# MLP hidden columns moved to the place of the second expert matrices, those loaded in halves, and the last token tiles grouped three and one

## The chip, the cores and the metric

One core of one Trainium2 chip runs the whole program. The metric is the device time of one launch in microseconds (us), the median of several runs; lower is better. Engines are named as in the profile: PE is TensorE (matmuls; PEld its weight loads), DVE is VectorE, ACT is ScalarE, POOL is GpSimd, and SP is the engine that issues most DMAs.

## The reference, cut to what matters

Four batches of 1024 tokens with 256 channels pass through two layers. Layer 0 is softmax attention and a low-rank feed-forward; layer 1 is a linear-attention block with an MLP inside, and then a mixture of small experts. The change concerns the end of the layer-1 block and the start of the experts:

```python
# inside the layer-1 attention block
x = attn_out + inputs
y = layer_norm(x, ln2_scale, ln2_bias)
y = jax.nn.gelu(y @ w1 + b1) @ w2 + b2          # w1: 256x1024, w2: 1024x256
return x + y
...
# the experts: of each 16 consecutive tokens, each of 16*4 slots chooses one
grouped = x.reshape(x.shape[:-2] + (-1, ne, d))
logits = jnp.einsum('...btd,des->...btes', grouped, controller)
perm = (logits == jnp.max(logits, axis=-3, keepdims=True)).astype(x.dtype)
sel = jnp.einsum('...btd,...btes->...besd', grouped, perm)
inner = jax.nn.relu(jnp.einsum('...besd,desf->...besf', sel, f1) + bias)
inter = jnp.einsum('...besf,esfd->...besd', inner, f2)
out = jnp.einsum('...besd,...btes->...btd', inter, perm)
```

`f1` and `f2` are 4 MB each and are loaded anew for each batch. Between the MLP and the experts stands another normalisation with a per-batch scale and shift, applied to every token.

## The kernel before

`batch(b, carry)` writes out the work of one batch, in program order, into one list of steps per engine (`Lane.do`); `Lane.emit` then turns each list into instructions, and each step waits for the steps named as its predecessors. So each engine is strictly in order, and the order of the calls in `batch` is the order on every engine. SP's list holds DMA issues; all of them go to one hardware queue (q1 of the profile).

The 1024 tokens of a batch are 8 tiles of 128. `x`, `h` and `xn` hold token tiles [128 tokens, 256]. Two halves of 4 tiles are worked through one after the other in the MLP. Eight PSUM banks are handed out in rotation by `Banks.take()`; a bank may be taken again once the step given to `read_by` is done.

The stretch around the change, in program order with its lines:

- L1627: SP issues `load_f2` (L1493, two DMAs of 2 MB, each to 64 of the 128 partitions) once the last attention tile has been turned back. `f2` lies at the start of the slab (`OVERLAY`, 8 K words per partition).
- L1629 to L1638: `mlp_wide(half, ...)` makes the hidden columns `hid1` (1024 hidden channels as 8 blocks of 128 rows, by 512 tokens) with a GELU on ACT, `mlp_output(0, ...)` multiplies them by `w2` for tiles 0 to 3 and adds to `x` (`residual`, L1066 and L1068, both DVE), then `normalise`, `slot_rows_of` (DVE L1504, POOL L1506) and `mlp_wide(1, ...)`. `hid1` shares its memory with `sel`, the chosen rows, so no chosen row can be copied to `sel` before the last tile of the MLP has been multiplied.
- L1719 to L1752: tiles 4 to 7 of the MLP (`mlp_tile`, L1711, 8 products of 128x128 by 256, a generator that can be stopped in the middle) are mixed with the experts' choice for groups of tiles called LOW (0 to 3), MIDDLE (4, 5) and HIGH (6, 7). For each group: `norm_stats` (L297, L298, L300 on DVE, the power on POOL L301), `norm_apply` (L308), `slot_turn` (transposes L441, evacuated at L451 by ACT or L448 by DVE), `slot_rows_of`, `choices` (two products L470, three DVE passes L1521, L1525, L1526), `spread_choices` (transposes L1651, DVE L1655), `chosen_rows` for channel halves c=0 and c=1 (products L1685, copies to `sel` L1699 on ACT or L1701 on DVE; each call takes 4 banks) and `choice_blocks` (L1536). `hold_clock` puts spare transposes (L1667) on PE.
- L1758: SP issues `load_next`, the next batch's tokens `next_x` (two DMAs of 512 KB, to 128 partitions), once `choices(HIGH)` has been read from PSUM (`turned_read`). The last batch has none.
- L1763 to L1787: four blocks of the first expert product (L1773). After each block DVE adds the bias (L1779) and ACT takes the ReLU (L1786); after each addition, in the first three batches, DVE also takes the statistics of two tiles of `next_x` (L1784), which wait for all of `next_x`.
- L1790 to L1827: `rows_product(0)` and `rows_product(1)` (L1800), the first half of the second expert product; the first needs the ReLU of the first two blocks worked and all of `f2`, the second that of the last two. Then `second_product` (L1837), and the next batch's transposes.

The two statements in the stretch on which most hangs:

```python
            if b + 1 < NB:
                next_norm.update(norm_stats(next_x, n // 2, [NEXT_X] * 2, EPS, tiles=(2 * n, 2 * n + 1)))
...
            done = pe.do(emit, *[reader for i, ps, reader in taken.values()], inner_done[part_], inner_done[part_ + 2],
                         (loaded["f2"], 32 * (b + 1)))
```

Of the kernel before, what the change touches and what calls it, by code (L numbers as in the profile page):

```python
# [14 lines left out]
P = 128  # L15
NB = 4
S = 1024
# [95 lines left out]
def build(nc, I, out):  # L113
# [176 lines left out]
    def norm_stats(src, half, ready, eps, lanes=(dve, pool), filled=None, tiles=None):  # L290
# [4 lines left out]
        for pair, ready_ in zip(zip(tiles[0::2], tiles[1::2]), zip(ready[0::2], ready[1::2])):  # L295
# [3 lines left out]
            ts = slice(pair[0], pair[1] + 1, pair[1] - pair[0])  # L299
# [126 lines left out]
    def batch(b, carry):  # L426
# [671 lines left out]
        def gelu_into(dst, bias):  # L1098
            return lambda m, cols, ps, done: act.do(lambda e: nc.scalar.activation(
                dst[:, m, cols], ps, ACT.Gelu_apprx_tanh, bias=bias[:, m:m + 1]), done)  # L1100
# [347 lines left out]
        begin(WORK + 2 * S)  # L1448
        hid1 = part("hid1", [P, FM, S])
# [5 lines left out]
        def mlp_wide(half, turned):  # L1455
            return blocks(FM, lambda m, cols: [(w1[:, c, m * P:(m + 1) * P], mT[:, c, cols]) for c in range(C)], half, P,
                          gelu_into(hid1, b1_1), turned=turned)

        def mlp_output(half, wide, between=None):
            return to_residual(half, lambda tok: [(hid1[:, m, tok], w2[:, m, :]) for m in range(FM)], mod_rows[:, 4, :],  # L1460
                               wide=wide, ready=summed_x, between=between)

# [30 lines left out]
        def load_f2(e):  # L1493
            for k in range(2):
                last = e.dma_start(f2[k * EF:(k + 1) * EF, :, :], f2_dram[k]).then_inc(loaded["f2"], 16)
# [131 lines left out]
        sp.do(load_f2, last_turned)  # L1627
# [6 lines left out]
        LOW, MIDDLE, HIGH = tuple(range(TH)), (TH, TH + 1), (TH + 2, TH + 3)  # L1634
        mlp_turned = []
        slots_normed = [normalise(x, 0, mlp_output(0, wide0, lambda: mlp_turned.append(mlp_turn(1, mlp_norms[1]))), EPS)]
# [68 lines left out]
        def mlp_tile(t):  # L1705
# [4 lines left out]
            for m in range(FM):  # L1710
                done = pe.do(lambda e, m=m: nc.tensor.matmul(ps[:, 0:D], hid1[:, m, tok], w2[:, m, :], start=m == 0,  # L1711
# [6 lines left out]

        first_tile = mlp_tile(TH)  # L1719
# [4 lines left out]
        wrote4 = next(first_tile)  # L1724
        low_spread = spread_choices(LOW)
        *_, wrote5 = mlp_tile(TH + 1)
        middle_normed = norm_apply(x, norm_stats(x, 1, [wrote4, wrote5], EPS, tiles=MIDDLE))
        *_, wrote6 = mlp_tile(TH + 2)
        middle_turned = slot_turn(MIDDLE, middle_normed)
        middle_h = slot_rows_of(MIDDLE, middle_normed)  # L1730
        last_tile = mlp_tile(TH + 3)
        next(last_tile)
        choices(MIDDLE, middle_turned)
        wrote7 = next(last_tile)
        inv = norm_stats(x, 1, [wrote6, wrote7], EPS, tiles=HIGH)
        [*chosen_rows(LOW, (0,), [low_spread, *slots_h], ("act", "act", "act", "act"))]
# [229 lines left out]
```

## Time and profile before

| | us |
|---|---|
| median of 3 runs | 1734.58 (1732.05 to 1736.68) |
| the profiled execution | 1733.78 |
| its span | 1732.4 |

| engine | busy us | share of the span |
|---|---|---|
| PE | 1662.5 | 96% |
| PEld | 1133.2 | 65% |
| DVE | 1227.6 | 71% |
| POOL | 865.8 | 50% |
| ACT | 847.9 | 49% |

The profile divides the span among engines, gives the chain of work that ended last, and lists instructions by line. Shares of the whole span say little here: the four batches repeat one pattern of some 425 us, and the change touches some 40 us of each. The first expert product begins at 420.24, 845.64, 1271.11 and 1696.63 us of the span. All times quoted below are of the first batch unless said otherwise. "x4" behind a matmul line counts records; an fp32 product is recorded as two, a transpose as one.

### The profile page before, as it was taken

To read this page: it belongs to the slowest core of one execution; us is meant where nothing else is said; L and a number is where in the kernel's file an instruction comes from. 1 tells how busy PE (TensorE), PEld (TensorE's weight loads), DVE (VectorE), ACT (ScalarE), POOL (GpSimd) and SP (SyncE) were. 2 spreads that over 40 slices of the span, in tenths; PEclk is the share of its full clock that TensorE was granted. 3 is DMA by queue.
4 is the path that set the end of the run, shared out by engine and by line. 5 is a ranking of instruction groups with operands and counts; after the bars stand their busy time and mean duration, and the time that the engine had idled before them with its cause. 6 is when DMAs were issued, how large, how long until landed. Compare 5 with 4: busy or idle time off the path is not lost.

```text
span 1732.4 us, 41066 instructions
## 1 busy us (share of the span) xinstructions
PE 1662.5 (96%) x16518; PEld 1133.2 (65%) x16518; DVE 1227.6 (71%) x2678; ACT 847.9 (49%) x1864; POOL 865.8 (50%) x1123
## 2 busy tenths in 40 slices
PE   8999999999999999999999999999999999999997
PEld 5566685767566667566856667756684666766666
DVE  4988957626689994762678887675367999676545
ACT  5666634233577762422357765432245777443233
POOL 2788853141188884232128888314113888740410
PEclk9999999999999999999999999999999999999999
DMA  6566572141566655032346655405045666620504
GB/s 188 125 150 149 139 182 87 27 73 37 163 147 138 149 140 167 1 61 38 87 134 153 146 139 135 146 2 93 5 113 133 146 151 142 155 102 2 98 0 124
DMA packets 143853, 189.11 MB, mean 109 GB/s; under 512 B 34512, under 2 KB 107696, under 8 KB 142640
## 3 DMA queue, kind: packets, MB, share of 16 engines
q1 hardware_dynamic: 125472, 179.14, 42.1%
q10 hardware_dynamic: 18192, 7.35, 1.9%
q8 instruction: 131, 2.15, 0.6%
q14 instruction: 58, 0.48, 0.1%
HBM read 88.32 MB, written 13.16 MB: 59 GB/s over the span
## 4 chain that ended last, share of the span: by engine, by line
PE 61%; DVE 15%; ACT 6%; POOL 5%; SPq 5%; DMA 4%; issue 3%; POOLq 0%; ACTq 0%; DVEq 0%
PE scores L470 13%; PE bank L681 8%; PE scores L661 7%; SPq L1011 5%; PE bank L470 5%; DVE prob L800 5%; POOL placed L864 4%; DMA placed<-prob 4%; ACT prob L916 3%; PE bank L708 3%; PE scores L1711 2%; PE bank L718 2%; PE scores L1773 2%; PE scores L441 2%; PE scores L1368 1%
## 5 line engine op out<-in xcount | busy, mean ns | idle before, releaser
L864 POOL COPY placed<-prob 32x768 f32<-32x768 f32 x448 | 367.8, 821 | 216.7 <-DVE prob L800 186.0
L301 POOL TENSOR_TENSOR rstd<-rstd,minus_half 128x2 f32<-128x2 f32 x96 | 69.7, 728 | 506.9 <-DVE rstd L300 504.8
L681 PEld LDWEIGHTS bank<-placed,v_t 128*64 128x64 f32 x4608 | 250.7, 137 | 74.9 <-issue 73.2
L681 PE MATMUL bank<-placed,v_t 128*64 128x128 f32 x4608 | 272.6, 274 | 10.9 <-DMA placed<-prob 9.3
L661 PE MATMUL scores<-k_t,q_t 64*128 64x512 f32 (+3 forms) x1536 | 274.0, 496 | 1.1 <-DVE neg_max L793 1.0
L800 DVE STREAM_TRANSPOSE prob<-prob 128x1536 f32<-128x1536 f32 x128 | 222.5, 1764 | 46.7 <-ACT prob L916 46.5
L793 DVE CUSTOM_DVE_ANT_0 mod_rows<-scores,hx 128x128 f32<-128x128 f32 (+7 forms) x256 | 190.7, 745 | 32.1 <-PE scores L661 32.1
L661 PEld LDWEIGHTS scores<-k_t,q_t 64*128 64x128 f32 x1536 | 130.1, 187 | 112.9 <-issue 92.1
L864 POOL COPY placed<-hx 32x768 f32<-32x768 f32 x224 | 184.1, 822 | 33.3 <-DVE hx L800 16.6
L916 ACT ACTIVATE prob<-mod_rows,neg_max 128x128 f32<-128x128 f32 (+2 forms) x192 | 137.6, 717 | 117.6 <-DVE neg_max L793 113.9
L793 DVE CUSTOM_DVE_ANT_0 x<-scores,hx 128x128 f32<-128x128 f32 (+7 forms) x256 | 192.7, 753 | 0.0
L916 ACT ACTIVATE prob<-x,neg_max 128x128 f32<-128x128 f32 (+2 forms) x192 | 136.2, 709 | 0.0
L800 DVE STREAM_TRANSPOSE hx<-hx 128x1536 f32<-128x1536 f32 x64 | 112.0, 1749 | 6.1 <-ACT hx L916 6.1
L874 POOL TENSOR_TENSOR yT<-yT,inverse_wide 128x256 f32<-128x256 f32 (+2 forms) x128 | 91.4, 728 | 27.9 <-DMA inverse_wide<-inverse_scratch 21.4
L708 PE MATMUL bank<-hT,w_ring 128*64 128x512 f32 x448 | 101.5, 594 | 0.0
L1066 DVE TENSOR_TENSOR tmp<-bank,mod_rows 128x256 f32<-128x256 f32 x24 | 10.2, 424 | 125.8 <-PE bank L1122 71.5
L916 ACT ACTIVATE hx<-mod_rows,neg_max 128x640 f32<-128x640 f32 x64 | 59.9, 936 | 71.2 <-DVE neg_max L793 71.2
L470 PE MATMUL scores<-mT,w 128*128 128x512 f32 x192 | 85.4, 594 | 1.7 <-ACT mT L451 1.7
L924 ACT COPY yT<-bank 128x256 f32<-128x256 f32 (+2 forms) x128 | 44.1, 370 | 80.9 <-PE bank L681 80.7
L718 PE MATMUL bank<-w_ring,latT 128*64 128x128 f32 x1024 | 67.4, 275 | 3.4 <-ACT k_t L902 2.7
L451 ACT ACTIVATE hT<-scores,mod_cols 128x512 f32<-128x512 f32 (+1 forms) x40 | 26.8, 710 | 88.6 <-PE scores L441 88.6
L718 PEld LDWEIGHTS bank<-w_ring,latT 128*64 128x64 f32 x1024 | 57.2, 137 | 16.1 <-ACT k_t L902 8.9
(252 smaller groups left out, 3111.4 us busy)
## 6 DMA issues: line engine op xcount, KB each, us to landing
placed<-prob SPq DMA_DIRECT2D x576, 96.0 KB, 2.5
f<-in_L_ffn_f SPq DMA_DIRECT2D x16, 2048.0 KB, 13.6
placed<-hx SPq DMA_DIRECT2D x288, 96.0 KB, 2.2
inverse_wide<-inverse_scratch SPq DMA_DIRECT2D x64, 256.0 KB, 4.3
slots_scratch<-high_rows SPq DMA_DIRECT2D x16, 512.0 KB, 6.6
inter<-slots_scratch SPq DMA_DIRECT2D x32, 256.0 KB, 4.7
mod_rows<-mod_scratch SPq DMA_DIRECT2D x32, 128.0 KB, 5.0
out<-x SPq DMA_DIRECT2D x16, 256.0 KB, 2.1
```

The lines of the kernel that those rows point to most:

```text
L301: step = pool.do(lambda e, ts=ts: nc.gpsimd.tensor_tensor(rstd[:, ts], rstd[:, ts], minus_half[:, ts], op=ALU.pow), var, filled)
L470: step = pe.do(lambda e, n=n, w=w, m=m: nc.tensor.matmul(ps, w, m, start=n == 0, stop=n == len(pieces) - 1), copy, *after)
L661: last = nc.tensor.matmul(score_tiles[head][:, at_ // 512, at_ % 512:at_ % 512 + hi - lo], q_t[buf][rows_, tile * P:(tile + 1) * P], k_t[b ...
L681: last = nc.tensor.matmul(out_bank[rows_, at_:at_ + P], v_t[pair % 2][:, j, rows_], placed[m % 2][:, :, head, first_block(m, i) + j, :], s ...
L708: last = nc.tensor.matmul(ps[side, :], ring[:, c * P + side.start:c * P + side.stop], hT[:, c, cols], start=c == 0, stop=c == C - 1)
L718: last = nc.tensor.matmul(ps[side, t * P:(t + 1) * P], latT[:, at_ + side.start:at_ + side.stop], ring[:, 3 * P:4 * P], start=True, stop=True)
L793: nc.vector.tensor_tensor_reduce(masked_scores[head][:, cols], score_tiles[head][:, :, :].rearrange("p a n -> p (a n)")[:, cols], future[: ...
L800: nc.vector.transpose(p_, p_).then_inc(flow["shuffled"], 1)
L864: nc.gpsimd.tensor_copy(placed[m % 2][target * GROUP:(target + 1) * GROUP, source, :, :, :], prob[m % 3][source * GROUP:(source + 1) * GRO ...
L874: last = nc.gpsimd.tensor_tensor(dst, dst, out_place(m, lo, hi, inverse_wide), op=ALU.mult)
L916: nc.scalar.activation(prob[m % 3][:, :, head, blocks_in(m, i), :], masked_scores[head][:, columns_in(m, i)].rearrange("p (n g i) -> p g n ...
L1011: e.dma_start(placed[m % 2][target * GROUP:(target + 1) * GROUP, source, :, :, :], prob[m % 3][source * GROUP:(source + 1) * GROUP, target ...
```

## The change

`hid1` moves from the place of `sel` to that of `f2` and is laid out by halves. `f2` is loaded in two halves of its slots (4 DMAs of 1 MB instead of 2 of 2 MB): the first half after tile 3's MLP output, the second after that of tile 7. The chosen rows of tiles 0 to 3 for c=0 are multiplied and copied between the two halves of tile 6's MLP product, those for c=1 after `choices(MIDDLE)`. MIDDLE becomes tiles 4, 5, 6 and HIGH tile 7; HIGH's two channel halves come in one call. `choice_blocks(MIDDLE)` moves behind all chosen rows.

```diff
@@ norm_stats
-        for pair, ready_ in zip(zip(tiles[0::2], tiles[1::2]), zip(ready[0::2], ready[1::2])):
+        for pair, ready_ in [(tiles[k:k + 2], ready[k:k + 2]) for k in range(0, len(tiles), 2)]:
...
-            ts = slice(pair[0], pair[1] + 1, pair[1] - pair[0])
+            ts = slice(pair[0], pair[-1] + 1, max(pair[-1] - pair[0], 1))
@@ hid1
-        begin(WORK + 2 * S)
-        hid1 = part("hid1", [P, FM, S])
+        begin(OVERLAY)
+        hid1 = part("hid1", [P, NH, FM, HW])
+        begin(WORK + 10 * S)
         mT = part("mT", [P, C, S])
...
+        def mlp_hidden(m, tok):
+            half, at_ = tok.start // HW, tok.start % HW
+            return hid1[:, half, m, at_:at_ + P]
@@ load_f2
-        def load_f2(e):
+        def load_f2(e, half):
+            qs = slice(half * EP // 2, (half + 1) * EP // 2)
             for k in range(2):
-                last = e.dma_start(f2[k * EF:(k + 1) * EF, :, :], f2_dram[k]).then_inc(loaded["f2"], 16)
+                last = e.dma_start(f2[k * EF:(k + 1) * EF, qs, :], f2_dram[k][:, qs, :]).then_inc(loaded["f2"], 16)
             return last
@@ after the attention
-        sp.do(load_f2, last_turned)
...
-        LOW, MIDDLE, HIGH = tuple(range(TH)), (TH, TH + 1), (TH + 2, TH + 3)
+        LOW, MIDDLE, HIGH = tuple(range(TH)), (TH, TH + 1, TH + 2), (TH + 3,)
         mlp_turned = []
-        slots_normed = [normalise(x, 0, mlp_output(0, wide0, lambda: mlp_turned.append(mlp_turn(1, mlp_norms[1]))), EPS)]
+        outputs0 = mlp_output(0, wide0, lambda: mlp_turned.append(mlp_turn(1, mlp_norms[1])))
+        low_output = outputs0[-1]
+        slots_normed = [normalise(x, 0, outputs0, EPS)]
@@ the tiles 4 to 7
+        sp.do(lambda e: load_f2(e, 0), low_output)
         first_tile = mlp_tile(TH)
         next(first_tile)
         choices(LOW, low_turned)
         choice_blocks(LOW)
         act.do(lambda e: nc.scalar.activation(spare_column[:, :], minus_half[:, 0:1], ACT.Exp))
         wrote4 = next(first_tile)
+        *_, wrote5 = mlp_tile(TH + 1)
+        inv = norm_stats(x, 1, [wrote4, wrote5], EPS, tiles=MIDDLE[0:2])
         low_spread = spread_choices(LOW)
-        *_, wrote5 = mlp_tile(TH + 1)
-        middle_normed = norm_apply(x, norm_stats(x, 1, [wrote4, wrote5], EPS, tiles=MIDDLE))
-        *_, wrote6 = mlp_tile(TH + 2)
+        middle_normed = norm_apply(x, inv)
+        third_tile = mlp_tile(TH + 2)
+        next(third_tile)
+        [*chosen_rows(LOW, (0,), [low_spread, *slots_h], ("act", "act", "act", "act"))]
+        wrote6 = next(third_tile)
+        middle_normed += norm_apply(x, norm_stats(x, 1, [wrote6], EPS, tiles=MIDDLE[2:]))
+        last_tile = mlp_tile(TH + 3)
+        next(last_tile)
         middle_turned = slot_turn(MIDDLE, middle_normed)
         middle_h = slot_rows_of(MIDDLE, middle_normed)
-        last_tile = mlp_tile(TH + 3)
-        next(last_tile)
+        wrote7 = next(last_tile)
+        sp.do(lambda e: load_f2(e, 1), wrote7)
+        inv = norm_stats(x, 1, [wrote7], EPS, tiles=HIGH)
         choices(MIDDLE, middle_turned)
-        wrote7 = next(last_tile)
-        inv = norm_stats(x, 1, [wrote6, wrote7], EPS, tiles=HIGH)
-        [*chosen_rows(LOW, (0,), [low_spread, *slots_h], ("act", "act", "act", "act"))]
+        [*chosen_rows(LOW, (1,), [], ("act", "act", "act", "act"))]
+        high_normed = norm_apply(x, inv)
         middle_spread = spread_choices(MIDDLE)
-        choice_blocks(MIDDLE)
-        high_normed = norm_apply(x, inv)
-        second_low = chosen_rows(LOW, (1,), [], ("act", "act", "act", "act"))
-        next(second_low)
         high_turned = slot_turn(HIGH, high_normed, shared=True)
         high_h = slot_rows_of(HIGH, high_normed)
-        [*second_low]
+        [*chosen_rows(MIDDLE, (0,), [middle_spread, *middle_h], ("act", "act", "act", "dve"))]
         turned_read = choices(HIGH, high_turned)
-        middle_rows = chosen_rows(MIDDLE, (0, 1), [middle_spread, *middle_h], ("act", "act", "dve", "dve"))
+        middle_rows = chosen_rows(MIDDLE, (1,), [], ("act", "act", "act", "dve"))
         next(middle_rows)
         high_spread = spread_choices(HIGH)
         [*middle_rows]
-        [*chosen_rows(HIGH, (0,), [high_spread, *high_h], ("act", "dve", "act", "dve"), held=6)]
-        [*chosen_rows(HIGH, (1,), [], ("dve", "act", "dve", "act"))]
+        [*chosen_rows(HIGH, (0, 1), [high_spread, *high_h], ("act", "dve", "act", "dve"), held=6)]
+        choice_blocks(MIDDLE)
         choice_blocks(HIGH)
@@ rows_product
-                         (loaded["f2"], 32 * (b + 1)))
+                         (loaded["f2"], 64 * (b + 1)))
```

## Rows read from the trace of the kernel before

**Rows 1.** The page: busy tenths and granted clock in 40 slices

```profile
PE   8999999999999999999999999999999999999997
PEclk9999999999999999999999999999999999999999
```

**Rows 2.** Chain of work, MLP tiles to first expert product: start us, us, what

```profile
395.56 0.46 PE scores L1651 x4
396.01 7.10 PE scores L1711 x32
...
408.39 0.43 DVE tmp L1066
408.85 0.42 DVE x L1068
409.27 0.35 DVE stats L297
...
410.63 0.71 POOL rstd L301
411.37 0.42 DVE hx L308
...
418.05 0.38 PE scores L1685 x2
...
420.24 7.61 PE scores L1773 x256
427.86 1.03 PE scores L1800 x32
...
431.51 1.93 PE scores L1837 x32
```

**Rows 3.** Timeline of PE: start us, us, engine, line, what, idle before

```profile
388.84 1.04 PE L441 MATMUL scores<-ident,hx 128*128 128x128 f32 x8
389.72 1.89 PE L1711 MATMUL bank<-w,hid 128*128 128x256 f32 x8
409.38 0.33 PE L1651 MATMUL scores<-ident,permT 64*128 64x64 f32 x2
```

**Rows 4.** Timeline of DVE in the same stretch

```profile
396.86 0.68 DVE L1655 TENSOR_TENSOR perm<-scores,par_mask 128x512 f32<-128x512 f32 x1
...
414.31 0.42 DVE L1521 TENSOR_TENSOR logits<-scores,tie 128x256 f32<-128x256 f32 x1 [0.35 <-PE scores L470]
```

**Rows 5.** Timeline of ACT: copies of the chosen rows of tiles 0-3

```profile
410.00 1.57 ACT L1699 COPY sel<-scores 128x512 f32<-128x512 f32 x3
```

**Rows 6.** Issues by SP's queue: start us, us, line, what

```profile
339.66 2.62 SPq L1495 DMA_DIRECT2D f<-in_L_ffn_f  x2
414.76 0.94 SPq L271 DMA_DIRECT2D next_x<-in_L_attn_x  x2
```

**Rows 7.** Issue to landing: f2's two DMAs, then next_x's two

```profile
DMA to landing us min/median/max: 13.6/18.8/24.1
...
DMA to landing us min/median/max: 4.5/5.0/5.5
```

**Rows 8.** Stretches of f2's stream and next_x's: ..., clock, DMA share, GB/s

```profile
353.00:363.00 10.00, 10.00 (x30) 5.51 (x29) 0.13 (x1) 3.44 (x5) 7.12 (x10) 1.00 1.10 184
417.00:418.00 1.00, 0.71 (x16) 0.52 (x16) 1.00 (x4) 0.35 (x2) 0.00 (x0) 1.00 1.07 369
```

**Rows 9.** Timelines of DVE and ACT beside the first expert product

```profile
422.91 0.42 DVE L297 BATCH_NORM_STATS2 stats<-next_x 128x6 f32<-128x256 f32 x1
...
424.19 0.68 DVE L1779 TENSOR_TENSOR hx<-scores,fbias 128x512 f32<-128x512 f32 x1
...
428.65 0.63 ACT L1786 ACTIVATE inner<-hx 128x512 f32<-128x512 f32 x1 [1.24 <-DVE hx L1779]
```

**Rows 10.** A longer idle of PE, last batch: timeline, then a stretch's granted clock

```profile
1722.02 1.67 PE L1895 MATMUL scores<-inter,blockT 128*32 128x256 f32 x16 [2.15 <-DMA inter<-slots_scratch]
...
1723.00:1724.00 1.00, 0.68 (x8) 0.00 (x0) 0.27 (x1) 0.00 (x0) 0.00 (x0) 0.50 1.14 329
```

More of the change, by code:

```diff
@@ L1096, in blocks, with gelu_into @@
             return res
-        def gelu_into(dst, bias):
+        def gelu_into(dst, bias, place):
             return lambda m, cols, ps, done: act.do(lambda e: nc.scalar.activation(
-                dst[:, m, cols], ps, ACT.Gelu_apprx_tanh, bias=bias[:, m:m + 1]), done)
+                dst[:, m, place], ps, ACT.Gelu_apprx_tanh, bias=bias[:, m:m + 1]), done)
         def modulated_rows(half, inv, scale, shift):
@@ L1456, in mlp_wide @@
             return blocks(FM, lambda m, cols: [(w1[:, c, m * P:(m + 1) * P], mT[:, c, cols]) for c in range(C)], half, P,
-                          gelu_into(hid1, b1_1), turned=turned)
+                          gelu_into(hid1[:, half, :, :], b1_1, slice(0, HW)), turned=turned)
         def mlp_output(half, wide, between=None):
-            return to_residual(half, lambda tok: [(hid1[:, m, tok], w2[:, m, :]) for m in range(FM)], mod_rows[:, 4, :],
+            return to_residual(half, lambda tok: [(mlp_hidden(m, tok), w2[:, m, :]) for m in range(FM)], mod_rows[:, 4, :],
                                wide=wide, ready=summed_x, between=between)
+        def mlp_hidden(m, tok):
+            half, at_ = tok.start // HW, tok.start % HW
+            return hid1[:, half, m, at_:at_ + P]
         begin(OVERLAY)
@@ L1710, in mlp_tile @@
             for m in range(FM):
-                done = pe.do(lambda e, m=m: nc.tensor.matmul(ps[:, 0:D], hid1[:, m, tok], w2[:, m, :], start=m == 0,
+                done = pe.do(lambda e, m=m: nc.tensor.matmul(ps[:, 0:D], mlp_hidden(m, tok), w2[:, m, :], start=m == 0,
                                                              stop=m == FM - 1), reader, wide1[m])
```

## The prediction

> **What bounds the kernel now.** The page comes first: PE is busy nine tenths or more in nearly every slice, at full granted clock [rows 1], so time is to be had only where PE stands still or does spare work. The chain of waits is read next, for the stretch that the change touches. In it, the reader is to see two parts. From 396.01 to 408.36 us PE's MLP products carry the chain. From 408.39 to 420.24 us, from the last MLP product to the first expert product, it runs through small steps of four engines: residual, statistics, the power on POOL, the normalisation, transposes, choice, spread, chosen rows, copies [rows 2]. I call this the tail; it lasts 11.9 us, and four batches have it. Behind it PE alone sets the pace: first expert product 7.6 us, the two row products 3.65 us, then the second product, from 431.51 us [rows 2]. That second part has two conditions that cost nothing today: all of f2 has landed long ago, since its issue was at 339.66 us [rows 6] and its slower DMA landed 24.1 us after its own issue [rows 7], and next_x, issued at 414.76 us [rows 6], has landed at the latest 5.5 us after its issue [rows 7], about 420.7 us, when DVE first reads it at 422.91 us [rows 9]. The slack is 2.2 us. SP's queue must be read for these, not the engines' busy time.
>
> **The tail, step by step** (first batch; the start at 389.88 us is unmoved). Prices: half a tile's product 1.73 us (396.01 to 403.12 is two tiles in 7.1 us) [rows 2, 3]; a transpose 0.11 (8 in 0.87 from 388.84 us) [rows 3]; 16 row products 1.02 (408.36 to 409.38 us) [rows 2, 3]; from an MLP product's end to the written tile 0.90 (408.36 to 409.27 us) [rows 2]; a pair's statistics up to POOL's start 1.36 (409.27 to 410.63), for one tile 0.35 + 0.19 less, 0.82 [rows 2]; POOL and the hand-over 0.74, a normalisation 0.42 [rows 2]; a DVE pass 0.68 for 512 columns and 0.42 for 256 [rows 4], so 0.55 for 384 and 0.29 for 128 by the same slope, an estimate. The change keeps all products; it reorders them.
>
> Tile 4 ends at 395.07 us, tile 5 follows at once and ends at 398.52. Its rows are written at 399.42, the pair's statistics are done at 400.73, and only then does DVE's queue reach the spread of LOW's choice, which ends at 401.41. PE has meanwhile done the spread's transposes (0.44) and half of tile 6, until 400.7: it stands 0.7 us for the spread, a new wait. Behind it in PE's queue stand the LOW products and the rest of tile 6; ACT is the only one to wait for them. LOW c=0 ends at 402.45, tile 6 at 404.2, written at 405.1, normalised at 405.1 + 0.82 + 0.74 + 0.42 = 407.1. Half of tile 7 ends at 405.93, then MIDDLE's six transposes wait for tile 6: a second new wait of 1.1 us. They end at 407.55, tile 7 at 409.28, and it is written at 410.2 us, 0.9 us later than before. One LOW group of 1.02 us and one wait of 1.1 have come in ahead of it, MIDDLE's choice of 0.86 has gone behind it.
>
> The rest is shorter. Statistics of one tile and the power end at 411.7. DVE is then in MIDDLE's choice (three passes of 384 columns, 410.95 to 412.7), so the normalisation ends at 413.05, not at 412.1. ACT copies LOW c=1 from 411.7 to 413.8 (four copies at 0.52) [rows 5], then the HIGH transposes' first half until 414.25. MIDDLE's spread on DVE ends at 413.7, its c=0 products at 414.5, HIGH's choice on PE at 414.9. DVE first copies its share of MIDDLE (until 415.2), then makes the three passes of HIGH at 128 columns: 415.5 is where HIGH's logits are read, 416.1 where the choice stands. Spread transposes 0.3, DVE 0.3; the HIGH products start at 417.0. From the last group's start to the first expert product took 2.19 us (418.05 to 420.24) [rows 2] for as many products and the 12 spare transposes; that stays, as the copies (four of 128 columns on each of two engines, some 0.9 us) fit under it. So the first expert product starts at F = 419.2 us, 1.0 us earlier. The copying of LOW is no longer in the tail, but ACT was not what the tail waited for; the chain's small steps are, and their number is unchanged. MIDDLE's three copies on ACT cost nothing while they hide beside HIGH's choice. The later choice_blocks hide under the first expert product; uncovered they would cost under 1 us. The new layout of hid1 has the same rows and strides within a product: nothing, and 0.1 us per batch either way at the most, since its 8 products and GELUs keep their shapes.
>
> **The loads.** f2's first half is issued at some 378 us with SP idle and no user for 40 us: free. The second half can't be issued before tile 7 is written, at 410.2 us, 70 us later than all of f2 today. 2 MB on this path take 13.6 us to landing (f2's first DMA) [rows 7]; the stream behind it runs at 184 GB/s with all engines busy [rows 8]. Two DMAs of 1 MB keep 64 partitions and 1 KB pieces, so I take 13.6: landed at 423.85 us. The row products need it at F + 7.6 = 426.8: 3 us to spare. Bounds: 8.5 us if it flowed like next_x (369 GB/s) [rows 8], 14.7 with another issue.
>
> Next_x is what is late next. SP issues it behind f2, at 415.5 us, when 8 us of f2 are still in the queue. The two f2 DMAs landed one after the other (13.6 and 24.1 us) [rows 7], so a queue's DMAs go in order, and next_x lands 1.05 MB at 369 to 389 GB/s, 2.75 us, behind f2: N = 426.6 us. In three of four batches DVE's statistics of next_x stand between the first and second bias addition. DVE would be there at F + 2.67 = 421.9 us [rows 2, 9] and waits 4.7 us. Queued behind on DVE are the other three bias additions, hence ACT's ReLUs, hence both row products, hence PE. From DVE's first statistics to the last ReLU's end it is 6.37 us (422.91 to 429.28) [rows 9]; the second row product starts at N + 6.4 and ends 1.75 later, N + 8.15 = 434.75 us, where before it ended at 431.51 [rows 2]: 3.24 us per batch. What follows is paced by PE, so nothing gives it back. The last batch has no next_x and gains 1.0.
>
> The Trainium skill (SBUF — State Buffer, Door 1: The DMA port swizzle) says that partitions 0 to 63 reach only half of the 16 ports on SBUF's DMA side, and so do 64 to 127; half rate is what the trace shows. By its figure (half of 436 GB/s, an estimate) 2 MB would take 9.6 us where the trace has 11, and the sum would be 4.5 us less. The skill (DMA: Bandwidth & Descriptors, Queues, rings and completion order) adds that each DMA engine takes one queue's descriptors in ring order but alternates between queues; by that rule, with which the two landings agree, next_x would escape only from another queue, and the change has it on SP's.
>
> **Sum.** 3 x 3.24 - 1.04 = +8.7 us on the profiled execution's 1733.8: 1742.5. That execution lies 0.8 us under the median, so 1743.3.
>
> **Rivals.** (1) *The second half of f2 is early enough*: faster side. The point is fixed: next_x must land before 421.9 us, so f2 within 8.9 us of its issue. For it: smaller DMAs, next_x's rate of 369 GB/s, or next_x overtaking inside the queue. Against it: four batches' f2 loads all behaved alike, at half that rate. Then 4 x 1.04 is gained: 1730.4. (2) *The tail gains nothing*: if the new PE waits and ACT's queue eat the 1.0 us, only the last batch changes, as N does not depend on F: 3 x 3.24 = 9.7, 1744.3; it would also mean that the LOW copies between MLP tiles don't shorten anything. (3) *PE's clock falls*: PE idles 2.4 us ahead of the first row product. After an idle of 2.15 us the granted clock was 0.50 (1.2 GHz) a microsecond later [rows 10]. The first row product at half speed would only fill the wait for the last ReLU; I take 1 us more per batch: 1746.3. (4) *Better than reckoned ahead*: had I overstated the two new PE waits by 0.9 us, tile 7 is written at 409.3, N falls by 0.9, F is 2 us earlier: 3 x 2.34 - 2.0 = +5.0, 1739.6.
>
> **How the numbers follow.** Chances: the forecast 0.55, (1) 0.20, (2) 0.07, (3) 0.08, (4) 0.10. This kernel's measurement can tell about 0.3%, 5.2 us, from no change: bounds 1729.4 and 1739.8. Slower: 0.51 of the forecast's 0.55 (the rest if N is over 1.2 us earlier), (2), (3), 0.02 of (4): 0.68. Same: 0.04 + 0.08 of (1) + 0.08 of (4) = 0.20. Faster: 0.12, the part of (1) in which the tail gains over 1.3 us. The range reaches from 1731 (most of rival 1) to 1747 (rival 3); the forecast's own is 1739 to 1746.
>
> **What would show it.** In the profile after: tile 7 written near 410.2 and the first expert product near 419.2 us; PE idle ahead of the half-transposes of MIDDLE; f2's last DMA landing near 424, next_x's 11 us after its issue; DVE waiting some 4.7 us for a DMA ahead of L1784's statistics in three batches, not in the fourth; PE idle ahead of both row products, released by ACT. Wrong it is if DVE's statistics of next_x follow the bias addition at once, or if PE's waits ahead of the row products end with f2's DMA.

## The result, and the profile after

The changed kernel takes 1751.41 us (median of 4 runs, 1750.16 to 1754.31) against 1734.58 us of before: 16.8 us more, and the recorded ratio is 1.0102, interval 1.0089 to 1.0114. (Before's number is the median of three runs; a fourth, of 2135.92 us, fell in a slower state that the chip has and is left out.) It is slower by about twice what was forecast. Its profiled execution took 1750.16 us, span 1748.8 us.

The page of the changed kernel, engines' busy time, granted clock by slices and PE's instruction queue (packets, MB, share):

```profile
PE 1670.0 (95%) x16518; PEld 1140.5 (65%) x16518; DVE 1227.3 (70%) x2674; ACT 851.4 (49%) x1872; POOL 868.1 (50%) x1127
...
PEclk9999999999999999999999999999999999999998
...
q8 instruction: 131, 2.15, 0.5%
```

PE has as many matmuls as before and is busy 7.5 us longer, so some of them ran slower; the other 9 us of the span are idle time. The page says no more than that. The stretch of the first batch on PE, to be held against [rows 2, 3] (by the chain of work its tile 4 starts at 385.63 us, that of before at 389.88; the timelines have both some 0.17 us earlier):

```profile
397.10 0.39 PE L1692 MATMUL scores<-perm,hx 32*128 32x128 f32 x3 [0.53 <-DVE perm L1662]
...
403.11 0.66 PE L441 MATMUL scores<-ident,hx 128*128 128x128 f32 x4 [0.97 <-DVE hx L308]
...
409.07 0.37 PE L1658 MATMUL bank<-ident,permT 64*128 64x64 f32 x3 [1.18 <-DVE permT L1532]
...
412.98 0.88 PE L1674 MATMUL scores<-ident 128*128 128x128 f32 x6
...
415.90 0.97 PE L1784 MATMUL scores<-sel,f 128*64 128x64 f32 x25
419.29 8.62 PE L1784 MATMUL scores<-sel,f 128*64 128x64 f32 x231 [2.41 <-issue]
427.84 1.10 PE L1811 MATMUL scores<-f,inner 64*64 64x128 f32 x32
...
430.17 1.98 PE L1811 MATMUL scores<-f,inner 64*64 64x128 f32 x64 [0.36 <-ACT inner L1797]
432.08 2.00 PE L1848 MATMUL scores<-inner,f 64*128 64x64 f32 x32
```

The first three are the new idles of the reordering; two were foreseen. The line at 419.29 was not: after 25 records of the first expert product PE stands 2.41 us with "issue" as the reason, that is, for nothing that a semaphore shows. Behind it 231 records take 8.6 us, where before 256 took 7.6 [rows 2]. The wait for the last ReLU, which the prediction made the whole loss, is there too, at 430.17, with 0.36 us. Small as it is, it is the wait that ends last in this batch: the chain of work, followed back from the second product, doesn't go through PE's idle but through next_x.

```profile
412.48 11.15 DMA next_x<-in_L_attn_x
...
423.65 0.44 DVE stats L297
...
429.40 0.64 ACT inner L1797
...
430.17 1.98 PE scores L1811 x64
```

The second batch shows PE's idle larger, and with it the clock (stretches: busy time of PE, PEld, DVE, ACT, POOL, then granted clock, DMA share, GB/s):

```profile
845.83 2.49 PE L1784 MATMUL scores<-sel,f 128*64 128x64 f32 x77
852.20 7.01 PE L1784 MATMUL scores<-sel,f 128*64 128x64 f32 x179 [3.88 <-issue]
...
850.00:852.00 2.00, 0.00 (x0) 0.00 (x0) 0.00 (x0) 0.00 (x0) 0.00 (x0) 1.00 0.98 314
...
854.00:855.00 1.00, 1.00 (x24) 1.00 (x22) 0.93 (x4) 0.00 (x0) 0.00 (x0) 0.50 0.00 0
```

PE stands 3.88 us while the DMA engines are full, and works on at a granted clock of 0.50 (1.2 GHz), as it did behind the idle of [rows 10]. The 179 records took 7.0 us where before they took 5.3: 1.7 us more. Here the chain does go through the idle:

```profile
848.32 3.88 issue
852.20 7.01 PE scores L1784 x179
859.21 1.03 PE scores L1811 x32
```

DVE and SP's queue, to be held against [rows 6, 7, 9]: next_x waited for in the first and second batch; the issues of f2's second half and next_x; issue to landing of f2's four DMAs of the first batch and of next_x's in all three:

```profile
423.65 0.43 DVE L297 BATCH_NORM_STATS2 stats<-next_x 128x6 f32<-128x256 f32 x1 [1.42 <-DMA next_x<-in_L_attn_x]
...
853.88 0.43 DVE L297 BATCH_NORM_STATS2 stats<-next_x 128x6 f32<-128x256 f32 x1 [5.22 <-DMA next_x<-in_L_attn_x]
...
406.44 1.31 SPq L1501 DMA_DIRECT2D f<-in_L_ffn_f  x2
412.04 0.94 SPq L271 DMA_DIRECT2D next_x<-in_L_attn_x  x2
...
DMA to landing us min/median/max: 8.0/10.3/13.8
...
DMA to landing us min/median/max: 8.8/10.2/11.5
```

next_x does land behind f2, at 423.62 us, and DVE does wait for it. That all four batches lose can be seen in one table, worked out from the timelines of PE (us; A is the start of tile 4's product, F the first expert product, R the first row product, E the second product):

| | F - A | R - F | E - R | E - A | PE idle in the first product |
|---|---|---|---|---|---|
| before, batches 1, 2, 4 | 30.45 | 7.6 | 3.65 | 41.72 | 0 |
| after, batch 1 | 30.44 | 11.94 | 4.24 | 46.62 | 2.41 |
| after, batch 2 | 30.43 | 13.31 | 3.65 | 47.39 | 3.88 |
| after, batch 3 | 33.17 | 9.88 | 3.66 | 46.71 | 1.95 |
| after, batch 4 | 31.70 | 8.70 | 3.65 | 44.05 | 0.82 |

(Before's third batch has 41.94.) The losses in E - A are 4.9, 5.7, 4.8 and 2.3 us, together 17.7. By columns that is 13.4 us in the first product (9.1 of idle, 4.3 of slower records), 4.0 in the tails of batches 3 and 4, and 0.4 in the row products. The stretches between the batches' changed parts are 0.7 us longer in sum and the end of the program 2.3 us; against that this execution reached its first tile 4 4.3 us earlier. That last is luck: over all the profiles of this case tile 4 starts anywhere from 385.5 to 389.7 us, whether f2 is loaded early or late. 17.7 + 0.7 + 2.3 - 4.3 = 16.4 us, the difference of the spans.

**Where PE stops.** If PE stands for want of instructions, the idle must lie at fixed places of its program. Queue q8 of the page carried 131 packets of instructions, 2.15 MB, so 16 KB each; PE has 33,574 records (weight loads, matmuls and the few others), which is 131 times 256 and 38 more. I numbered the records in the order of the trace and took each idle put down to issue inside the first expert product ("remainder" is what is left of the number when divided by 256):

| kernel | batch | idle us | records ahead of it | remainder by 256 |
|---|---|---|---|---|
| after | 1 / 2 / 3 / 4 | 2.41 / 3.88 / 1.95 / 0.82 | 7361 / 15809 / 24257 / 32449 | 193 / 193 / 193 / 193 |
| loads_only | 1 / 2 / 3 / 4 | 2.96 / 2.58 / 3.11 / 2.14 | 7361 / 15809 / 24257 / 32449 | 193 / 193 / 193 / 193 |
| narrow_beside | 1 / 2 / 3 | 3.21 / 1.50 / 2.55 | 7617 / 16065 / 24257 | 193 / 193 / 193 |
| wide_beside | 1 / 2 / 3 | 0.74 / 0.94 / 2.00 | 7617 / 16065 / 24257 | 193 / 193 / 193 |

Fourteen idles in four different kernels, and all at the same remainder: they are the borders of blocks of 256 instructions. PE has used up its blocks there and the next has not come. The other experiments with a stream beside the first product (two_queues, late_statistics and next_x_late) have eight more, all at remainder 193.

The trace also holds the packets of q8, and they show the block coming. In all 22 cases PE goes on 1.2 to 1.6 us after one such packet has ended: at 419.28 us after the packet of 416.29 to 417.70, at 852.20 after that of 849.66 to 850.79. These packets took 1.0 to 1.5 us, no longer than those of the kernel before (0.9 to 1.65). So the block isn't moved slowly; it starts late. In the kernel before, the packet that belongs to a border inside the first product had ended 1.4 to 4.0 us ahead of it: the spare time was thin already. The Trainium skill (Runtime: NRT & Kernel Launch, Instruction fetch mechanics) describes such blocks of 16 KiB, 256 instructions, fetched by DMA while the ones before are executed, and calls their cost mostly hidden. The traces agree on the block; hidden it is only as long as the DMA engines are free.

### The profile page after: what moved, and what is told of

It is laid out like the page before. It is cut to its first block, busy times and chain, and to the rows that moved or that the text cites. A ratio compares the mean times of both kernels' runs of the same rounds, so it can differ in the third digit from the quotient of the medians.

```text
span 1748.8 us, 41074 instructions
## 1 busy us (share of the span) xinstructions
PE 1670.0 (95%) x16518; PEld 1140.5 (65%) x16518; DVE 1227.3 (70%) x2674; ACT 851.4 (49%) x1872; POOL 868.1 (50%) x1127
## 3 DMA queue, kind: packets, MB, share of 16 engines
q8 instruction: 131, 2.15, 0.5%
## 4 chain that ended last, share of the span: by engine, by line
PE 64%; DVE 15%; ACT 5%; SPq 5%; POOL 4%; DMA 4%; issue 3%; ACTq 0%; POOLq 0%; DVEq 0%
PE scores L470 13%; PE bank L681 9%; PE scores L661 7%; PE bank L470 5%; SPq L1011 4%; DVE prob L800 4%; ACT prob L916 3%; POOL placed L864 3%; PE bank L708 2%; DMA placed<-prob 2%; PE bank L718 2%; PE bank L712 2%; DVE stats L297 2%; DVE hx L800 2%; PE scores L1784 1%
## 5 line engine op out<-in xcount | busy, mean ns | idle before, releaser
L301 POOL TENSOR_TENSOR rstd<-rstd,minus_half 128x2 f32<-128x2 f32 (+1 forms) x100 | 71.5, 716 | 523.1 <-DVE rstd L300 521.0
L1066 DVE TENSOR_TENSOR tmp<-bank,mod_rows 128x256 f32<-128x256 f32 x28 | 11.9, 423 | 128.7 <-PE bank L1122 70.7
L708 PEld LDWEIGHTS bank<-hT,w_ring 128*64 128x64 f32 x448 | 31.6, 137 | 53.3 <-issue 53.3
## 6 DMA issues: line engine op xcount, KB each, us to landing
f<-in_L_ffn_f SPq DMA_DIRECT2D x8, 2048.0 KB, 11.5
```

The costliest lines, as they stand in the source:

```text
L301: step = pool.do(lambda e, ts=ts: nc.gpsimd.tensor_tensor(rstd[:, ts], rstd[:, ts], minus_half[:, ts], op=ALU.pow), var, filled)
L708: last = nc.tensor.matmul(ps[side, :], ring[:, c * P + side.start:c * P + side.stop], hT[:, c, cols], start=c == 0, stop=c == C - 1)
```

## The experiments

Ratios are to before, measured beside each. The theories at the start: LOADS, in two parts (NEXT_X, the predicted wait, and STARVATION, PE without instructions), against ORDER.

**order_only**: the new order of the tiles, without the late load.

```diff
-        begin(OVERLAY)
+        begin(WORK + 2 * S)
         hid1 = part("hid1", [P, NH, FM, HW])
...
+        sp.do(load_f2, last_turned)
-        sp.do(lambda e: load_f2(e, 0), low_output)
-        sp.do(lambda e: load_f2(e, 1), wrote7)
```

> The changed order of the tiles and chosen rows alone: the MLP's hidden columns lie by halves in the place of the chosen rows, as before (half 0 where channel half c=0 of them goes, so it can be written between MLP tiles), and f2 is loaded whole and early, as before. Theory LOADS (the late second half of f2 costs everything: next_x queued behind it, and PE short of instructions while the stream runs): 1735 to 1737 us, PE idle nowhere inside the first expert product. Theory ORDER (PE's new idle of 1.2 us ahead of MIDDLE's spread lowers the clock, as seen in batches 3 and 4 of the change): 1738 to 1741 us, with a granted clock near 0.5 in the tail.

Measured 1738.48 us, ratio 1.0014 (1.0002 to 1.0026), 10 runs. E - A is 41.73, 42.94, 41.72 and 41.73 us, no idle in the first expert product. So the order neither gains nor costs in three batches; in the second one PE was busy 1.6 of the 3 us from 836, a gap of 1.2 us among them, and the clock fell in the tail:

```profile
840.00:841.00 1.00, 1.00 (x17) 0.86 (x20) 0.68 (x3) 0.44 (x2) 0.00 (x0) 0.50 0.06 16
```

The median lies in theory ORDER's range, and the fallen clock is what ORDER said; but it is 2.7 us of a loss of some 17, so LOADS must account for nearly all.

**loads_only**: the order of before, hidden columns in f2's place, f2 in halves.

```diff
-        sp.do(load_f2, last_turned)
+        sp.do(lambda e: load_f2(e, 0), low_output)
...
         wrote7 = next(last_tile)
+        sp.do(lambda e: load_f2(e, 1), wrote7)
```

> The order of before, with hidden columns in f2's place and f2 loaded in halves, the second after tile 7's output. Theory LOADS: tile 7 is written 1.4 us earlier than in the change, f2 and next_x need some 17 us from there, so the second product starts some 3.5 us late in three batches, or later where PE runs short of instructions: 1745 to 1750 us, idle of 1 to 4 us put down to issue inside the first expert product in all four batches. Theory ORDER: 1735 to 1740 us.

Measured 1750.84 us, ratio 1.009 (1.0073 to 1.0107), just above the range of LOADS. F - A is 30.46 in all batches, so nothing is lost ahead of the first product; E - A is 45.33, 46.07, 45.52 and 44.19. In the first batch:

```profile
419.45 0.92 PE L1782 MATMUL scores<-sel,f 128*64 128x64 f32 x24
423.32 6.99 PE L1782 MATMUL scores<-sel,f 128*64 128x64 f32 x232 [2.96 <-issue]
```

The loads alone make nearly the whole loss, the last batch (which has no next_x) with 2.5 us too. That batch can't be NEXT_X's. The first three could: their second products start 8.5, 9.3 and 9.3 us behind next_x's landing, and next_x_late below measures what that wait takes by itself, 8.46 us.

**no_second_half**: the change without the second load (the products read f2's first half in its place, so half of the second matrices is left out).

```diff
-        sp.do(lambda e: load_f2(e, 1), wrote7)
...
-                                                         inner[rows_, q, :], f2[rows_, q, P:D], start=True, stop=True)
+                                                         inner[rows_, q, :], f2[rows_, q % (EP // 2), P:D], start=True, stop=True)
```

> The change without the load of f2's second half; the products read the first half in its place (it leaves out half of the second expert matrices). Both parts of theory LOADS: 1735 to 1738 us, next_x landing 5 us after its issue, no idle inside the first expert product. If the stream of f2 is not the cause: still near 1751 us.

Measured 1738.83 us, ratio 1.0019 (1.0009 to 1.0029): the same as order_only. E - A is 41.73, 42.94, 42.99, 41.72; next_x lands 3.8 to 5.5 us behind its issue again. The stream is the cause. Two batches lose the 1.2 us of the clock, which puts the time 0.8 us over the expected range.

**late_statistics**: the change with next_x's statistics out of the bias additions' way.

```diff
-            if b + 1 < NB:
-                next_norm.update(norm_stats(next_x, n // 2, [NEXT_X] * 2, EPS, tiles=(2 * n, 2 * n + 1)))
...
         for part_ in range(2):
             rows_product(part_)
+            for n in (2 * part_, 2 * part_ + 1) if b + 1 < NB else ():
+                next_norm.update(norm_stats(next_x, n // 2, [NEXT_X] * 2, EPS, tiles=(2 * n, 2 * n + 1)))
```

> The change with the statistics of next_x moved behind the row products' copies, so that no bias addition waits for next_x. If the wait for next_x carries the loss, as predicted: 3 x 3 to 5 us less than the change, 1737 to 1742 us. If PE's idle inside the first expert product (2.4, 3.9, 2.0 and 0.8 us in the change's trace) and the halved clock behind it carry it, the wait for next_x being hidden under them: only 0.5 to 2 us less than the change, 1749 to 1751 us.

Measured 1760.76 us, ratio 1.0144: 9 us slower than the change, outside both expectations. E - A is 46.06, 47.42, 47.49 and 43.99 against the change's 46.62, 47.39, 46.71 and 44.05: taking the wait for next_x away gives nothing, as PE's own idle beside it is as long (five idles at block borders, 11.1 us in sum). The loss came behind it: from the second product to the next batch's tile 4 the three stretches are 4.6, 3.2 and 4.3 us longer than in the change. Of that 1.2 us is PE waiting for the normalisation on DVE ahead of the next batch's transposes (8.0 against 6.8 us ahead of L441); the rest was not traced. The experiment settles what it was for, E - A; as a repair it is none.

**next_x_late**: before, with next_x issued some 7.5 us later and no other stream.

```diff
-            sp.do(load_next, turned_read)
...
+            if n == 0 and b + 1 < NB:
+                sp.do(load_next, done)
```

> The kernel before with next_x issued once PE has done the first block of the first expert product, some 7.4 us later than before and with no f2 stream: the price of a late next_x by itself. Its landing is then some 5 us behind the issue, N = F + 7.1 against F + 2.67 where DVE wants it. Theory NEXT_X (the prediction's chain holds: DVE, bias additions, ReLUs, row products): the second product starts at F + 15.2 to 15.9 instead of F + 11.3 in three batches, not in the fourth: 1746 to 1750 us, PE idle ahead of the row products. If the chain has slack that the prediction missed: under 1740 us.

Measured 1752.61 us, ratio 1.0096 (1.0074 to 1.0117), above the expected range. In the first batch, on DVE and on PE:

```profile
426.87 0.43 DVE L297 BATCH_NORM_STATS2 stats<-next_x 128x6 f32<-128x256 f32 x1 [4.58 <-DMA next_x<-in_L_attn_x]
...
429.60 1.10 PE L1798 MATMUL scores<-f,inner 64*64 64x128 f32 x32 [2.45 <-ACT inner L1784]
...
433.39 1.98 PE L1798 MATMUL scores<-f,inner 64*64 64x128 f32 x64 [1.81 <-ACT inner L1784]
435.30 2.00 PE L1835 MATMUL scores<-inner,f 64*128 64x64 f32 x32
```

This is the predicted chain undisturbed: next_x waited for, both row products released by ACT's ReLUs, E - A 46.30, 47.14 and 46.24 us, the last batch 41.73. In all three batches the second product starts 8.46 us behind next_x's landing (the prediction said 8.15). The mechanism and its price hold.

With that number the change can be taken apart. next_x landed at 423.62, 853.86 and 1284.83 us; 8.46 us behind, the second product could start at 432.1, 862.3 and 1293.3, and it did at 432.08, 862.79 and 1294.12. So in the first batch the wait for next_x ended last and PE's idle was hidden beside it; in the second and third PE itself was later, by 0.5 and 0.8 us (in the third the tail, 2.7 us late, has its share). The wait alone would have cost 4.9, 5.2 and 3.9 us (an estimate, landing plus 8.46 against before), and late_statistics shows that without it PE's idle costs about as much: its E - F is 14.3, 17.0 and 15.8 us in these batches, against 11.3 before. Two causes, each nearly enough for the whole loss of these batches, ran side by side.

Two things more stand in this trace. In the third batch PE stands 1.19 us at a block border: a late next_x by itself is a stream that can starve it. And in the second batch the granted clock fell to 0.50 at the end of PE's idle of 3.30 us ahead of the first row product, the place that rival 3 named, yet the second product started 8.46 us behind the landing there too: it cost nothing ahead of it.

**narrow_beside** and **wide_beside**: before, with 1 MB more read into dead rows beside the first expert product in the first three batches, to 64 partitions at a time (narrow, the first DMA below) or to 128 (wide, the second).

```diff
             sp.do(load_next, turned_read)
+            sp.do(load_beside, sel_product[-1])
...
+        def load_beside(e):
+            for k in range(2):
+                last = e.dma_start(h[k * EF:(k + 1) * EF, :, :], f2_dram[k][:, 0:T, :]).then_inc(loaded["beside"], 16)
...
+                last = e.dma_start(h[:, ts, :], x_in[b][:, ts, :]).then_inc(loaded["beside"], 16)
```

> The kernel before with 1 MB of f2 read once more, to 64 partitions at a time, into the then dead rows of h, issued behind next_x once the last chosen rows are multiplied, so that it streams some 5.5 us beside the first expert product; only the next batch's clearing of that place waits for it. Theory STARVATION (a stream on the DMA engines keeps PE's instructions away by itself): idle of 1 to 3 us inside the first expert product in each batch, no engine waiting for a semaphore there, 1741 to 1750 us. If only waits for next_x and f2 cost: 1735 to 1737 us.

> The same as narrow_beside with 1 MB written to all 128 partitions (the rows that next_x also reads), which flows twice as fast. Theory STARVATION by a stream held up at its destination: little or no idle in the first expert product, 1735 to 1738 us. If any busy DMA engines starve PE: idle of about half of narrow_beside's, 1738 to 1743 us.

Measured 1744.86 us, ratio 1.005 (1.0035 to 1.0066), and 1738.61 us, ratio 1.002 (1.0009 to 1.0031). No step of the first product waits for the extra megabyte, and next_x lands as before; yet PE stands in the first expert product, here the first batch of each:

```profile
417.80 3.38 PE L1779 MATMUL scores<-sel,f 128*64 128x64 f32 x110
424.39 4.66 PE L1779 MATMUL scores<-sel,f 128*64 128x64 f32 x104 [3.21 <-issue]
```

```profile
424.32 3.25 PE L1780 MATMUL scores<-sel,f 128*64 128x64 f32 x104 [0.74 <-issue]
```

The idles are 3.21, 1.50 and 2.55 us narrow and 0.74, 0.94 and 2.00 us wide; the fourth batch, without the extra load, has none. (The profiled execution of wide_beside was the slowest of its ten, 1743.54 us, so its idles may be more than usual.) A stream by itself starves PE, and for longer when it is the narrow one, which lands 7.6 to 8.9 us behind its issue against 5.2 to 6.7. The rival (only a stream held up at its destination does it) falls: the wide one does it too.

**two_queues**: the change with the upper half's DMA issued by ACT.

```diff
-        sp.do(lambda e: load_f2(e, 1), wrote7)
+        sp.do(lambda e: load_f2(e, 1, (0,)), wrote7)
+        act.do(lambda e: load_f2(e, 1, (1,)), wrote7)
```

> The change, but of the second half of f2 the DMA for partitions 64 to 127 is issued from ACT's queue, the one for 0 to 63 from SP's, both once tile 7 is written. If a stream to 64 partitions is held at 190 GB/s by the place it writes to, the two together flow at up to 380 GB/s, f2 is in after 8 us instead of 13.6, next_x with it, and PE has its instructions again before the first expert product: 1737 to 1742 us. If the rate is set by how f2 is read, nothing changes: 1749 to 1752 us.

Measured 1743.35 us, ratio 1.0052 (1.0031 to 1.0073): half of the loss is gone, a little less than expected. f2's two DMAs of the first batch, and a stretch in which both flow:

```profile
DMA to landing us min/median/max: 8.0/10.0/11.9
...
414.00:417.00 3.00, 2.79 (x40) 2.29 (x33) 1.83 (x8) 2.02 (x7) 0.00 (x0) 1.00 1.12 275
```

The last landing is at 11.9 us instead of 13.8, next_x lands 6.2 to 8.6 us behind its issue instead of 8.8 to 11.5, and the idles in the first product are 0.88, 0, 0.76 and 0. That stretch has some of next_x in it; from 412.0 to 413.6 us, ahead of next_x's issue, f2's two DMAs alone had 292 GB/s. The stream in one queue stays at 194 to 201 GB/s in the change. One queue isn't the limit either, as next_x gets 369 GB/s in one [rows 8]. So the narrow stream is limited by the partitions that it writes. E - A is still 2.2 to 2.7 us over before in three batches.

**order_held**: order_only, 8 spare transposes in the gap ahead of MIDDLE's spread.

```diff
-        middle_spread = spread_choices(MIDDLE)
+        middle_spread = spread_choices(MIDDLE, held=8)
```

> order_only with 8 spare transposes of PE in the 1.35 us gap ahead of MIDDLE's spread, so that PE has no idle there. Theory CLOCK (the 1.2 us that one batch of order_only and two of no_second_half lost ahead of the first expert product, and the 2.7 and 1.3 us of the change's third and fourth batch, are that gap's): all four batches reach the first expert product 30.4 to 30.6 us after tile 4's start with the granted clock at 1.00, and the median falls by 1 to 3 us, to 1735 to 1737.5 us. Otherwise: one or two batches still late, 1738 to 1739 us.

Measured 1733.84 us, ratio 0.9989 (0.998 to 0.9999): 4.6 us under order_only by the medians, more than expected and more than the 1.2 us that order_only's one trace shows at this place. F - A is 30.38 or 30.39 in all four batches, so the 1.2 us of single batches, and the 2.7 and 1.3 us of the change's third and fourth, belong to the gap: in the change the third batch ran its tail at 0.50 from 1273 us on. The gap is in every batch, the lower clock only in some.

**retuned** and **retuned_less_held**: order_only, with the chosen rows of tiles 0-3 and the MIDDLE transposes behind tile 7, 8 or 2 spare transposes ahead of MIDDLE's spread, and 3 instead of 6 ahead of HIGH's products. Against order_only:

```diff
-        third_tile = mlp_tile(TH + 2)
-        next(third_tile)
-        [*chosen_rows(LOW, (0,), [low_spread, *slots_h], ("act", "act", "act", "act"))]
-        wrote6 = next(third_tile)
+        *_, wrote6 = mlp_tile(TH + 2)
...
         last_tile = mlp_tile(TH + 3)
         next(last_tile)
-        middle_turned = slot_turn(MIDDLE, middle_normed)
         middle_h = slot_rows_of(MIDDLE, middle_normed)
         wrote7 = next(last_tile)
         inv = norm_stats(x, 1, [wrote7], EPS, tiles=HIGH)
-        choices(MIDDLE, middle_turned)
-        [*chosen_rows(LOW, (1,), [], ("act", "act", "act", "act"))]
+        middle_turned = slot_turn(MIDDLE, middle_normed)
         high_normed = norm_apply(x, inv)
-        middle_spread = spread_choices(MIDDLE)
-        high_turned = slot_turn(HIGH, high_normed, shared=True)
+        [*chosen_rows(LOW, (0,), [low_spread, *slots_h], ("act", "act", "act", "act"))]
+        choices(MIDDLE, middle_turned)
+        second_low = chosen_rows(LOW, (1,), [], ("act", "act", "act", "act"))
+        high_turned = slot_turn(HIGH, high_normed)
         high_h = slot_rows_of(HIGH, high_normed)
-        [*chosen_rows(MIDDLE, (0,), [middle_spread, *middle_h], ("act", "act", "act", "dve"))]
+        [*second_low]
+        middle_spread = spread_choices(MIDDLE, held=8)
         turned_read = choices(HIGH, high_turned)
+        [*chosen_rows(MIDDLE, (0,), [middle_spread, *middle_h], ("act", "act", "act", "dve"))]
...
-        [*chosen_rows(HIGH, (0, 1), [high_spread, *high_h], ("act", "dve", "act", "dve"), held=6)]
+        [*chosen_rows(HIGH, (0, 1), [high_spread, *high_h], ("act", "dve", "act", "dve"), held=3)]
```

> The groups of 3 and 1 tiles on top of order_only (f2 whole and early, hidden columns by halves in the chosen rows' place), with the chosen rows of tiles 0-3 put back behind tile 7, where PE only waited for the normalisation, the MIDDLE transposes behind tile 7 too, and 8 spare transposes ahead of MIDDLE's spread. By the rows of before, PE loses no time ahead of tile 7 (written 1.6 us earlier than before, 3 us earlier than in the change), and the tail keeps its shortening by one tile: the first expert product 2 to 3.4 us earlier than before in all four batches: 1722 to 1728 us. If the tail's gain is illusory: 1733 to 1736 us.

> retuned with 2 instead of 8 spare transposes ahead of MIDDLE's spread. In retuned DVE waited 1.01 us for that spread, whose transposes stood behind the 8 spare ones although the choice was there. The spread comes some 0.7 us earlier, and everything behind it: first expert product 27.8 to 28.0 us after tile 4's start instead of 28.55, 1722 to 1724 us. If another wait takes its place (ACT's copies of tiles 0-3): 28.3 to 28.55 us and no change, 1724 to 1726 us.

Measured 1725.23 us, ratio 0.9945 (0.9927 to 0.9962), and 1725.73 us, ratio 0.9936 (0.992 to 0.9953): both beat before and the change. How much of it the three spare transposes left out ahead of HIGH's products give was not measured by itself. In retuned, tile 7's product ends 16.3 us after A (before 18.6, after 20.0) and F - A is 28.55 in all batches; the first expert product runs through:

```profile
416.09 7.68 PE L1783 MATMUL scores<-sel,f 128*64 128x64 f32 x256
```

With fewer spare transposes F - A is 27.9, within the expectation, and the profiled span is 1723.3 us against 1726.3; but the median is where it was, above the expected 1722 to 1724 us, and the two medians don't tell the versions apart.

## Why the prediction was wrong

The direction was right, the size half of the measured: +8.7 us forecast, +16.8 by the medians and +17.7 by the ratio and by the table of E - A. Three steps of the sum failed. The first is the size of the wait for next_x: three batches at 3.24 us, 9.7 in sum, where the measured landings make it 4.9, 5.2 and 3.9, 14.0 in sum. The second is a term that it had at nothing: PE's own supply of instructions. It adds little to these three batches only because it runs beside the wait; taking the wait away gave nothing back. The third is the last batch, forecast 1.0 us faster and 2.3 slower. The missing 9.0 us are 4.3 of the first, 1.3 by which PE was later than the wait in batches 2 and 3, and 3.4 of the last batch.

- **The tail.** Forecast: first expert product 1.0 us earlier. Measured: 0.0 in batches 1 and 2 (30.44 against 30.45), later in 3 and 4. The step that failed is the sum of small terms: tile 7 was written 20.8 us after tile 4's start, not 20.3 (the LOW group took 1.17, not 1.02, and the half tile behind it 1.94, not 1.73), HIGH's choice stood 27.0 us after it, not 26.2, and the HIGH products didn't wait for DVE's spread (done at 413.38) but for their own 6 spare transposes, which stood behind it in PE's queue (412.98 to 413.79 in the trace after); these I had left out. Rival 2 was nearer.
- **The idles of the reordering** were named, two of three with the right size (0.7 and 1.1 forecast, 0.53 and 0.97 measured). The third, 1.2 us ahead of MIDDLE's spread, was in the working's times but was not called an idle, and it is the one that lowers the clock in some batches.
- **f2 and next_x.** From tile 7's writing to next_x: forecast 16.4 us, measured 17.2 (406.43 to 423.62), and 17.5 and 16.4 in batches 2 and 3. With tile 7's 0.5 us, next_x came 1.3, 1.6 and 0.5 us later than forecast, counted from tile 4's start. The issue behind f2, the order in the queue and the halved rate all hold.
- **From next_x to the second product.** Forecast 8.15 us, measured 8.46 in the change's first batch and in all three of next_x_late. The mechanism was right and the term 0.3 us short. In the change's second and third batch it is not what ends last, by 0.5 and 0.8 us.
- **The missing term.** "They need f2 at F + 7.6: 3 us to spare" looked at f2 only through the steps that wait for it. That the same stream shares the DMA engines with PE's instruction blocks was not in the working at all. The idles are 2.41 + 3.88 + 1.95 + 0.82 = 9.1 us, with the halved clock behind two of them (1.7 us in the second batch). Most of this lies beside the wait for next_x and doesn't add to it. In the last batch, which has no such wait, it does: of the 2.3 us lost there 1.1 are the first product's (8.70 against 7.62 us) and 1.25 the tail's.
- **Rival 3** had the clock right and its place wrong: not behind the wait for the ReLUs but behind the starved PE, and in the tail. (next_x_late has it in the forecast place.)
- The lower gain of the LOW copies between MLP tiles has a plain reason, which retuned shows: before, they ran while PE waited for tile 7's normalisation (408.36 to 411.8 us) [rows 2]. Moved ahead of tile 7 they take PE's time at full price.

What stays open: why the stream keeps a 16 KB block away for 2 to 4 us. The traces show that the block's packet starts late and is then moved as fast as ever, not whether it waits behind packets of the stream or is asked for late. Why the clock fell in some batches at the same gap and not in others isn't settled either. The 2.3 us at the program's end appear in the change's profile and not in the other kernels' with late loads; one execution doesn't say what they are.

## What to carry to other kernels

A load has three kinds of users: the steps that wait for it, the loads queued behind it, and the engines whose instructions come over the same DMA engines; ask for all three, the last above all where PE runs short matmuls. The same stream stood beside PE's long products without an idle (30 matmuls in 10 us at 184 GB/s [rows 8]) and cost 0.7 to 3.9 us a batch beside a stretch of 256 records in 7.6 us. When two waits lie side by side, price each alone: removing one may give nothing back, as late_statistics did. And work that runs while an engine waits is free where it stands: before moving it forward, see whether it fills a wait.

## What the runs showed of the hardware

- PE's instructions come in blocks of 256, 16 KB each: the fourteen idles of the table and eight more lie at the same remainder, and PE went on 1.2 to 1.6 us behind the end of a block's packet. Beside a stream a block border cost 0.7 to 3.9 us; in the kernels without one the first expert product has no idle at its borders.
- 1 MB more in flight is enough for it, to 64 partitions (210 GB/s from 419 to 421 us of narrow_beside) and to 128 (317 GB/s in the same window of wide_beside) alike: 7.3 and 3.7 us of idle over three batches.
- A stream to 64 partitions flows at 184 to 201 GB/s in one queue (before and after); issued from two queues, to both sets of 64, f2's second half had 292 GB/s (two_queues, 412.0 to 413.6 us).
- The granted clock fell to 0.50 behind starved idles of 2.4 and 3.9 us in the change, yet not behind those of 2.96 and 3.11 us in loads_only, and in some batches behind a gap of 1.2 us; 8 spare transposes in that gap kept it at 1.00 in the tails of all four batches of order_held.
